# A two-layer attention and mixture-of-experts kernel: 23 tiles of expert rows in place of 24, with the last turn of each loop cut to three slots

## The chip, the cores and the metric

The kernel runs on one core of a Trainium2 chip. The time is the device time of one execution in microseconds (us), taken from the core. Several executions are made of each kernel and the median is given. The core has five engines, each with a queue of its own: PE (TensorE, matmuls), ACT (ScalarE), DVE (VectorE), POOL (GpSimd) and SP (SyncE, which here only issues transfers). They meet through semaphores alone.

## What is computed

x has 8 batches of 512 tokens with 128 channels, 4096 rows in all. Four layers follow each other, each added to x: a gated power attention, an expert layer, a delta rule layer, and the same expert layer again. The expert layer is the part that matters here:

```python
x = hidden_states.reshape(-1, c)                 # 4096 rows of 128
gates = softmax((x @ w_red) @ wg_n.T)            # 8 experts
idx = argmax(gates, axis=1)                      # one expert for each row
h = gelu(x @ w1[idx] + b1[idx])                  # 512 wide
out = (h @ w2[idx] + b2[idx]) * gates[idx]
```

## The kernel before

The function `experts` is called twice, with f = 0 (expert stage 0, some 430 to 560 us into the span) and f = 1 (expert stage 1, the last of the kernel, from about 960 us). In both, the rows are first sorted by expert into the DRAM tensor `xs_dram` by indirect transfers that POOL issues. Each expert has an area there, filled to a multiple of ST = 256 rows. A tile is 256 rows of one expert. How many tiles each expert has is known only on the chip, so DVE computes two tables of NS entries, `texp` (the expert of a tile) and `t_row` (its first row), and the program works on NS tiles whatever the routing is. With 4096 rows and 8 experts no routing needs more than floor((4096 + 8 * 255) / 256) = 23 tiles. NS is that number rounded up to a multiple of SLOTS = 4, which is 24. Entries past the last real tile name the last expert and rows of an idle area, and their results go to rows of `ys_dram` that nobody reads.

A tile is worked on in slot q of turn r: its number is 4r + q, and NR = 6 turns make the stage. All buffers that transfers fill (`xs`, `w1s`, `w2s`, `bs`, `yo`) have four slots. What one tile needs, engine by engine:

- SP, `rows(r, q)`: loads the tile's first row number into a register (L1387), waits until the slot's rows of four tiles ago were turned by PE (`x_ps`, L1389) and their row numbers were read by DVE (`who_done`, L1390), and issues the transfer of the rows (L1391). `weights(r, q)`: loads the expert's number (L1373), issues w1 (L1376), w2 (L1380) and the biases (L1382).
- PE, `turn_x` (L1786, two transposes), `up` (L1796), `down` (L1806), `turn_y` (L1817, two transposes). They are software-pipelined: one pass of `run` for slot q does `turn_x` of the next tile, `up` of this one, `turn_y` of the tile two back, and `down` of the tile one back.
- ACT copies the turned rows (`x_copy`, L1505) and makes the four GELUs (L1514).
- DVE, `y_bias` (L1692), then in `y_out` the two small operations that make the target rows (L1701 and L1704, which counts `who_done`), and the copy of the result (L1707).
- POOL, `give_back`: two indirect transfers to `ys_dram` (L1439).

The order is set by the queues alone. Each engine has the first turn written out, then a hardware loop (`Fori`) over the turns. On PE and ACT the last turn is written out again (`run(NR - 1, last=True)`), without `turn_x` in its last slot; PE then empties its pipeline with `turn_y`, `down` and `turn_y`. On SP, DVE and POOL the loop goes to the last turn. The lines of SP's loop:

```python
            with sp.Fori(0, NR - 1) as r:
                for q in range(SLOTS):
                    rows(r + 1, q, True)
                    weights(r + 1, q, True)
```

After stage 0 all engines meet at a barrier (L1276), and the delta rule layer reads all of `ys_dram`. After stage 1, SP waits for all four slots' `ys_out`, reads `ys_dram` back (L1414), DVE adds it to x (L1721), and x is stored (L1419).

Of the kernel before, what the change touches and what calls it, by code (L numbers as in the profile page):

```python
# [38 lines left out]
ST = 256  # L39
SLOTS = 4  # L40
NS = -(-((B * T + E * (ST - 1)) // ST) // SLOTS) * SLOTS
NR = NS // SLOTS
SPAN = SLOTS * ST
# [1231 lines left out]
def experts(nc, x, xs_dram, ys_dram, s, keep, f, w_red, wg, w1, b1, w2, b2, out):  # L1275
    with ExitStack() as ctx:  # L1276
# [91 lines left out]
        def _(sp):  # L1368
# [35 lines left out]
            rows(0, SLOTS - 1, f > 0)  # L1404
            with sp.Fori(0, NR - 1) as r:
                for q in range(SLOTS):
                    rows(r + 1, q, True)
                    weights(r + 1, q, True)

            if f == 1:  # L1410
                for q in range(SLOTS):
                    sp.wait_ge(ys_out[q], 16 * NC2 * NR * (f + 1))
                for k in range(B):
# [10 lines left out]
        def _(pool):  # L1424
# [16 lines left out]

            with pool.Fori(0, NR) as r:
                for q in range(SLOTS):
                    give_back(r, q)

        @block.scalar
        def _(act):
# [59 lines left out]
            def gelu(r, q, late=True):  # L1507
                g = NS * f + SLOTS * r + q
                act.wait_ge(s["h_ps"], g + 1)
                act.wait_ge(ws_in[q], 48 * (NR * f + r + 1))  # L1510
                if late:
                    act.wait_ge(s["y_ps"], g - 1)
                for n in range(NF):
                    ins = act.activation(hs[:, q % 2, n, :],  # L1514
                                         bH[:, 2 * (q % 2) + n // 2, ST * (n % 2):ST * (n % 2) + ST],
                                         ACT.Gelu, bias=bs[:, q, n:n + 1])
                ins.then_inc(s["h_sb"], 1)

            def run(r, late=True, last=False):
                for q in range(SLOTS):  # L1520
                    if not (last and q == SLOTS - 1):
                        x_copy(*before_slot(r, q, -1), late or q >= 1)
                    gelu(r, q, late or q >= 2)
# [8 lines left out]
        def _(dve):  # L1532
# [153 lines left out]
            def y_bias(r, q, late=True):  # L1686
                g = NS * f + SLOTS * r + q
                dve.wait_ge(s["y_ps"], g + 1)
                dve.wait_ge(ws_in[q], 48 * (NR * f + r + 1))
                if late:  # L1690
# [4 lines left out]
            def y_out(r, q, late=True):  # L1695
                g = NS * f + SLOTS * r + q
                if late:

                    dve.wait_ge(ys_out[q], 16 * NC2 * (NR * f + r))
                dve.wait_ge(xs_in[q], 16 * (NR * f + r + 1))  # L1700
                dve.tensor_scalar(aside[:, q, :], xs[:, q, :, C], float(B * T), float(ST * q), ALU.is_ge, ALU.mult)\  # L1701
# [8 lines left out]
            for q in range(SLOTS):  # L1710
                y_bias(0, q, late=f > 0 or q >= 2)
                y_out(0, q, late=f > 0)
            with dve.Fori(1, NR) as r:
                for q in range(SLOTS):
                    y_bias(r, q)
                    y_out(r, q)
            for i in range(NT if f == 1 else 0):
                if i % TT == 0:
# [6 lines left out]
        def _(pe):  # L1725
# [53 lines left out]
            def turn_x(r, q, late=True):  # L1779

                g = NS * f + SLOTS * r + q
                pe.wait_ge(xs_in[q], 16 * (NR * f + r + 1))
                if late:
# [5 lines left out]
            def up(r, q, late=True):  # L1789
                g = NS * f + SLOTS * r + q  # L1790
                pe.wait_ge(ws_in[q], 48 * (NR * f + r + 1))
                pe.wait_ge(s["x_sb"], g + 1)
# [27 lines left out]
            def run(r, first=False, last=False):  # L1820

                for q in range(SLOTS):
                    if not (last and q == SLOTS - 1):
                        turn_x(*before_slot(r, q, -1))
# [11 lines left out]
            run(NR - 1, last=True)  # L1836
            turn_y(NR - 1, SLOTS - 2)
            down(NR - 1, SLOTS - 1)
            turn_y(NR - 1, SLOTS - 1)


def delta_rule(nc, x, ys_out, ys, keep, row_in, row_done, counted, Wq, Wk, Wv, Wgamma, Wf, Wg1, Wg2, Wo, norm_w):
    with ExitStack() as ctx:
# [135 lines left out]
        def _(sp):  # L1979
            for q in range(SLOTS):  # L1980
                sp.wait_ge(ys_out[q], 16 * NC2 * NR)
            for k in range(B):
# [741 lines left out]
```

## Time and profile before

| | |
|---|---|
| median of 3 runs | 1151.78 us (1148.69 to 1154.24) |
| the profiled execution | 1151.33 us, its span 1149.5 us |
| mean granted clock of TensorE | 0.856 of full speed |
| PE busy (matmuls) | 853.0 us, 74% of the span |
| DVE busy | 761.6 us, 66% |
| POOL busy | 560.9 us, 49% |
| ACT busy | 536.1 us, 47% |

The span goes from the first to the last instruction; the profiled execution's own time lies 1.8 us above it. Busy shares are means over four layers with different limits. For this change only the two expert stages matter, so the rows further down come from these two stretches. A queue's name with a q (SPq) means the instructions of the engine's sequencer: issues of transfers, register and branch instructions.

### The profile page before, as it was taken

The page shows a single profiled execution, that of the slowest core. Times are in us where ns is not written, and L with a number is a line of the kernel's source. Part 1 is how long each engine was busy: PE and PEld are TensorE (multiplying, and loading weights), DVE is VectorE, ACT ScalarE, POOL GpSimd, SP SyncE. Part 2 cuts the span into 40 slices and gives each one's busy share as a digit, 9 for nine tenths or more (in the row PEclk, how much of TensorE's full clock was granted, in tenths as well). Part 3 has the DMA queues.
Part 4 walks back from the last instruction along what each step waited for, and adds up shares of the span by engine and source line. Part 5 has one row for each costly group of instructions (what it writes and reads, how often), then busy time and mean ns, then how long its engine had stood idle before and what let it go on. Part 6 is the DMA issues. An engine that isn't in the chain of part 4 may idle for free. (4 is left out here: it accounts for less than half of the span.)

```text
span 1149.5 us, 26726 instructions
## 1 busy us (share of the span) xinstructions
PE 853.0 (74%) x9326; PEld 630.0 (55%) x9326; DVE 761.6 (66%) x1722; ACT 536.1 (47%) x1219; POOL 560.9 (49%) x698
## 2 busy tenths in 40 slices
PE   3678888888888753999188999468678574629992
PEld 2455555656555533778124786156556463528781
DVE  7577687786877741222364889999999997612224
ACT  4577677576675722444055220255555531214440
POOL 4466557576575631444550010277777841534442
PEclk9998898798887966999688999878878985559997
DMA  5343141331413004666338400000020110156665
GB/s 161 112 155 98 60 162 46 125 109 59 161 52 119 11 11 139 180 186 185 102 60 106 74 1 0 0 1 0 0 73 0 36 38 10 38 156 171 189 191 165
DMA packets 129207, 101.80 MB, mean 89 GB/s; under 512 B 20640, under 2 KB 116832, under 8 KB 129056
## 3 DMA queue, kind: packets, MB, share of 16 engines
q1 hardware_dynamic: 120080, 87.27, 27.5%
q0 software_dynamic: 5120, 10.53, 2.7%
q10 hardware_dynamic: 3904, 2.61, 0.8%
q8 instruction: 68, 1.11, 0.4%
q14 instruction: 35, 0.29, 0.1%
HBM read 57.98 MB, written 35.45 MB: 81 GB/s over the span
## 5 line engine op out<-in xcount | busy, mean ns | idle before, releaser
L796 DVE TENSOR_SCALAR a_mag<-a_pS 128x1024 int32<-128x1024 int32 (+1 forms) x192 | 180.1, 950 | 65.1 <-PE a_pS L1155 63.2
L553 ACT ACTIVATE a_pw<-a_mag,a_eps_a 128x1024 f32<-128x1024 f32 (+1 forms) x192 | 175.5, 935 | 57.5 <-DVE a_mag L796 52.0
L1439 POOL DMA_INDIRECT ys_dram<-f_yo,f_who x96 | 91.9, 957 | 137.8 <-DVE f_yo L1707 121.1
L416 POOL TENSOR_TENSOR a_pw<-a_pw,a_decay 128x256 f32<-128x256 f32 x128 | 93.1, 728 | 104.7 <-ACT a_pw L553 104.3
L1155 PE MATMUL a_pS<-a_qf,a_kf 64*64 64x192 bf16 (+3 forms) x1536 | 111.2, 270 | 5.0 <-DVE a_mag L796 3.5
L1514 ACT ACTIVATE f_hs<-f_bH,f_bs 128x256 f32<-128x256 f32 x192 | 75.2, 474 | 67.5 <-issue 35.1
L2617 PE MATMUL d_c<-d_pb_p,ident 128*128 128x256 f32 x256 | 72.3, 452 | 41.9 <-POOL d_pb_p L2100 41.9
L1187 PE MATMUL a_pOff<-a_pw,a_vo 128*18 128x64 f32 x3584 | 97.1, 242 | 2.3 <-issue 2.3
L1796 PE MATMUL f_bH<-f_xsT,f_w1s 128*128 128x256 f32 x384 | 94.1, 389 | 0.0
L1692 DVE TENSOR_SCALAR f_ysT<-f_bY,f_bs 128x256 f32<-128x256 f32 x48 | 23.2, 484 | 106.9 <-PE f_bY L1806 87.6
L1806 PE MATMUL f_bY<-f_hs,f_w2s 128*128 128x256 f32 x384 | 90.8, 379 | 0.0
L2617 PEld LDWEIGHTS d_c<-d_pb_p,ident 128*128 128x128 f32 x256 | 58.6, 232 | 56.1 <-issue 39.0
L1155 PEld LDWEIGHTS a_pS<-a_qf,a_kf 64*64 64x64 bf16 x1536 | 65.3, 115 | 30.8 <-DVE a_mag L796 7.8
L2617 PE MATMUL d_c<-d_pb_d,ident 128*128 128x256 f32 (+1 forms) x256 | 64.8, 419 | 22.0 <-POOL d_pb_d L2100 22.0
L1187 PEld LDWEIGHTS a_pOff<-a_pw,a_vo 128*18 128x18 f32 x3584 | 69.2, 109 | 17.5 <-issue 13.9
L2094 POOL TENSOR_TENSOR d_pb_p<-d_Q,d_s_sb 128x512 f32<-128x512 f32 x32 | 37.3, 1166 | 83.1 <-ACT d_s_sb L2202 83.1
L1796 PEld LDWEIGHTS f_bH<-f_xsT,f_w1s 128*128 128x128 f32 x384 | 71.1, 195 | 9.1 <-issue 0.2
L1806 PEld LDWEIGHTS f_bY<-f_hs,f_w2s 128*128 128x128 f32 x384 | 69.2, 190 | 7.7
L2617 PEld LDWEIGHTS d_c<-d_pb_d,ident 128*128 128x128 f32 x256 | 53.2, 220 | 33.5 <-POOL d_pb_d L2100 24.8
L1707 DVE COPY f_yo<-f_bO 128x256 f32<-128x256 f32 x48 | 20.4, 425 | 71.9 <-PE f_bO L1817 57.1
L364 POOL TENSOR_TENSOR a_vo<-a_vd,a_reach 128x1008 f32<-128x1008 f32 (+6 forms) x56 | 65.9, 1191 | 1.1 <-issue 1.1
L2198 ACT ACTIVATE d_G<-d_c,d_g_ahead 128x64 f32<-128x64 f32 x64 | 24.0, 375 | 71.2 <-DVE d_og L2435 71.2
(395 smaller groups left out, 1837.6 us busy)
## 6 DMA issues: line engine op xcount, KB each, us to landing
parts_scratch<-a_parts SPq DMA_DIRECT2D x32, 384.0 KB
f_w1s<-in_L_ffn_w_dram SPq DMA_DIRECT2D x48, 256.0 KB
f_w2s<-in_L_ffn_w_dram SPq DMA_DIRECT2D x48, 256.0 KB
a_kf<-parts_scratch SPq DMA_DIRECT2D x16, 512.0 KB, 5.7
a_qf<-parts_scratch SPq DMA_DIRECT2D x16, 512.0 KB, 7.7
f_xs<-xs_dram SPq DMA_DIRECT2D x48, 129.0 KB
parts_scratch<-a_parts SPq DMA_DIRECT2D x16, 256.0 KB
xs_dram<-blank ACTq DMA_DIRECT2D x16, 129.0 KB
```

What stands on the lines that cost most here:

```text
L364: pool.tensor_tensor(vo[:, vo_at(j, j + 1):vo_at(j, j + 1) + n, :, :], vd[:, k, j, :, :].unsqueeze(1).broadcast_to([P, n, NP, 18]), reach[ ...
L416: pool.tensor_tensor(own, own, decay[:, k, m, hf:NP:2, :], ALU.mult)\
L553: act.activation(pw[:, n % 4, 0:N], mag[:, n % 3, 0:N], ACT.Square, bias=eps_a[:, 0:1])\
L796: dve.tensor_scalar(mag[:, n % 3, 0:2 * N].bitcast(I32).rearrange("p (l t) -> p l t", l=2), pS[:, 2 * (n % 2):2 * (n % 2) + 2, 0:N].bitcas ...
L1155: ins = pe.matmul(pS[lo:hi, 2 * (n % 2) + Q // 2, at:at + L * (end - first)], kf[lo:hi, k, p, L * m:L * m + L], qf[lo:hi, k, p, L * first: ...
L1187: ins = pe.matmul(pOff[lo:hi, L * i:L * i + L], vo[:, vo_at(m, i), p, :], wi, start=False, stop=(m == NM - 2), skip_group_check=True)
L1439: pool.indirect_dma_start(ys_dram[f][:, :], bass.IndirectOffsetOnAxis(ap=who[:, q, a:a + 1], axis=0), yo[:, q, a, :], None).then_inc(ys_ou ...
L1514: ins = act.activation(hs[:, q % 2, n, :], bH[:, 2 * (q % 2) + n // 2, ST * (n % 2):ST * (n % 2) + ST], ACT.Gelu, bias=bs[:, q, n:n + 1])
L1796: ins = pe.matmul(bH[:, 2 * (q % 2) + n // 2, ST * (n % 2):ST * (n % 2) + ST], w1s[:, q, P * n:P * n + P], xsT[:, q % 2, :], start=True, s ...
L1806: ins = pe.matmul(bY[:, 0:ST], w2s[:, q, n, :], hs[:, q % 2, n, :], start=(n == 0), stop=(n == NF - 1))
L2094: pool.tensor_tensor(po[:, 0:8], Q[:, :, :, bass.ds(c, 1)].rearrange("p k j c -> p k (j c)").unsqueeze(3) .broadcast_to([P, HD, CH, HD]), ...
L2617: ins = pe.matmul((c5, c6)[a][:, 0:64 * chunks].rearrange("p (c x) -> p c x", x=64), ident[:, :], po[:, k], start=(k == 0), stop=(k == 15))
```

## The change

NS becomes 23, without the rounding. NR stays 6 (rounded up), `LEFT` = 3 is the number of slots in the last turn, and `TURNS` = [6, 6, 6, 5] says how often each slot is used; it takes the place of NR in the counts that are waited for. The tables `texp` and `t_row` have 23 entries. In both expert stages SP's loop makes 4 turns in place of 5, POOL's 5 in place of 6, DVE's 4 in place of 5, and each is followed by three slots that are written out. PE and ACT keep their loops and lose the last slot of their last turn, which was written out before.

```diff
@@ -38,8 +38,10 @@
-NS = -(-((B * T + E * (ST - 1)) // ST) // SLOTS) * SLOTS
-NR = NS // SLOTS
+NS = (B * T + E * (ST - 1)) // ST
+NR = -(-NS // SLOTS)
+LEFT = NS - SLOTS * (NR - 1)
+TURNS = [NR if q < LEFT else NR - 1 for q in range(SLOTS)]
...
@@ -1402,14 +1404,17 @@
-            with sp.Fori(0, NR - 1) as r:
+            with sp.Fori(0, NR - 2) as r:
                 for q in range(SLOTS):
                     rows(r + 1, q, True)
                     weights(r + 1, q, True)
+            for q in range(LEFT):
+                rows(NR - 1, q, True)
+                weights(NR - 1, q, True)
...
-                    sp.wait_ge(ys_out[q], 16 * NC2 * NR * (f + 1))
+                    sp.wait_ge(ys_out[q], 16 * NC2 * TURNS[q] * (f + 1))
...
-            with pool.Fori(0, NR) as r:
+            with pool.Fori(0, NR - 1) as r:
                 for q in range(SLOTS):
                     give_back(r, q)
+            for q in range(LEFT):
+                give_back(NR - 1, q)
...
@@ -1517,8 +1524,8 @@
             def run(r, late=True, last=False):
-                for q in range(SLOTS):
-                    if not (last and q == SLOTS - 1):
+                for q in range(LEFT if last else SLOTS):
+                    if not (last and q == LEFT - 1):
                         x_copy(*before_slot(r, q, -1), late or q >= 1)
                     gelu(r, q, late or q >= 2)
...
@@ -1710,10 +1717,13 @@
-            with dve.Fori(1, NR) as r:
+            with dve.Fori(1, NR - 1) as r:
                 for q in range(SLOTS):
                     y_bias(r, q)
                     y_out(r, q)
+            for q in range(LEFT):
+                y_bias(NR - 1, q)
+                y_out(NR - 1, q)
...
@@ -1819,8 +1829,8 @@
             def run(r, first=False, last=False):
 
-                for q in range(SLOTS):
-                    if not (last and q == SLOTS - 1):
+                for q in range(LEFT if last else SLOTS):
+                    if not (last and q == LEFT - 1):
                         turn_x(*before_slot(r, q, -1))
...
             run(NR - 1, last=True)
-            turn_y(NR - 1, SLOTS - 2)
-            down(NR - 1, SLOTS - 1)
-            turn_y(NR - 1, SLOTS - 1)
+            turn_y(NR - 1, LEFT - 2)
+            down(NR - 1, LEFT - 1)
+            turn_y(NR - 1, LEFT - 1)
```

How the instructions stand at the end of expert stage 0. First PE, from `turn_x` of the third tile of the last turn on. The first instruction of each piece is shown, with the semaphores that it waits for (f_bA: `turn_x`, f_bH: `up`, f_bO: `turn_y`, f_bY: `down`). Before:

```order
L1786 MATMUL f_bA<-ident,f_xs 128x128 [waits f_x_sb,f_xs_in2]
L1796 MATMUL f_bH<-f_xsT,f_w1s 128x256 [waits f_h_sb,f_x_sb,f_ws_in1]
L1817 MATMUL f_bO<-ident,f_ysT 128x128 [waits f_o_sb,f_y_sb]
L1806 MATMUL f_bY<-f_hs,f_w2s 128x256 [waits f_y_sb,f_h_sb]
L1786 MATMUL f_bA<-ident,f_xs 128x128 [waits f_x_sb,f_xs_in3]
L1796 MATMUL f_bH<-f_xsT,f_w1s 128x256 [waits f_h_sb,f_x_sb,f_ws_in2]
L1817 MATMUL f_bO<-ident,f_ysT 128x128 [waits f_o_sb,f_y_sb]
L1806 MATMUL f_bY<-f_hs,f_w2s 128x256 [waits f_y_sb,f_h_sb]
L1796 MATMUL f_bH<-f_xsT,f_w1s 128x256 [waits f_h_sb,f_x_sb,f_ws_in3]
L1817 MATMUL f_bO<-ident,f_ysT 128x128 [waits f_o_sb,f_y_sb]
L1806 MATMUL f_bY<-f_hs,f_w2s 128x256 [waits f_y_sb,f_h_sb]
```

And after the change, from the same place:

```order
L1796 MATMUL f_bA<-ident,f_xs 128x128 [waits f_x_sb,f_xs_in2]
L1806 MATMUL f_bH<-f_xsT,f_w1s 128x256 [waits f_h_sb,f_x_sb,f_ws_in1]
L1827 MATMUL f_bO<-ident,f_ysT 128x128 [waits f_o_sb,f_y_sb]
L1816 MATMUL f_bY<-f_hs,f_w2s 128x256 [waits f_y_sb,f_h_sb]
L1806 MATMUL f_bH<-f_xsT,f_w1s 128x256 [waits f_h_sb,f_x_sb,f_ws_in2]
L1827 MATMUL f_bO<-ident,f_ysT 128x128 [waits f_o_sb,f_y_sb]
L1816 MATMUL f_bY<-f_hs,f_w2s 128x256 [waits f_y_sb,f_h_sb]
L1827 MATMUL f_bO<-ident,f_ysT 128x128 [waits f_o_sb,f_y_sb]
L1816 MATMUL f_bY<-f_hs,f_w2s 128x256 [waits f_y_sb,f_h_sb]
```

One pass of `turn_x`, `up`, `turn_y` and `down` is gone; the lines are later by 10 (one `up` and one `turn_x` with its wait for f_xs_in3 are missing), and the emptying of the pipeline has the same form.

Second SP, from the end of its loop in stage 0. Before, the loop's branch is followed by the branch to the barrier and by the delta rule layer's first transfers:

```order
L1382 ISA
L1382 DMA f_bs<-bT 128x5
L1405 REGISTER_ALU
L1405 COMPARE_AND_BRANCH
L1276 UNCONDITIONAL_BRANCH
L1978 UNCONDITIONAL_BRANCH [waits barrier_Pool_Activation_PE_DVE_SP_release]
L1983 DMA d_LL<-ys_dram 128x4x128 [waits f_ys_out2,f_ys_out3,f_ys_out1,f_ys_out0]
```

After the change, the loop's branch is followed by the first written-out slot (f_xs is the rows, f_w1s and f_w2s the weights, TENSOR_LOAD reads the table entry):

```order
L1384 ISA
L1384 DMA f_bs<-bT 128x5
L1407 REGISTER_ALU
L1407 COMPARE_AND_BRANCH
L1389 TENSOR_LOAD f_t_row
L1389 ISA x2
L1393 ISA [waits f_who_done,f_x_ps]
L1393 DMA f_xs<-xs_dram 128x2x129
L1375 TENSOR_LOAD f_texp
L1375 ISA x2
L1378 ISA [waits f_h_sb]
L1378 DMA f_w1s<-in_L_ffn_w_dram 128x512
```

The written-out slot has no REGISTER_ALU ahead of its table loads, since the entry's address is a constant; two more such slots follow it, and then the branch to the barrier.

## Rows read from the trace of the kernel before

**Rows 1.** Busy times by window: a stretch of each expert stage's loop

```profile
core 0: us, PE busy (x) PEld busy (x) DVE busy (x) ACT busy (x) POOL busy (x), PEclk, DMA share, GB/s
460.00:540.00 80.00, 76.33 (x382) 63.34 (x381) 22.14 (x77) 37.09 (x97) 36.37 (x38) 1.00 0.68 188
...
1023.00:1120.00 97.00, 90.85 (x444) 74.88 (x445) 23.77 (x84) 43.86 (x113) 38.31 (x40) 0.96 0.62 176
```

**Rows 2.** Timeline of PE, stage 0: `turn_x` (L1786) of tiles 19, 20 and 23

```profile
524.60 0.38 PE L1786 MATMUL f_bA<-ident,f_xs 128*128 128x128 f32 x2
...
529.31 0.43 PE L1786 MATMUL f_bA<-ident,f_xs 128*128 128x128 f32 x2 [0.65 <-DMA f_xs<-xs_dram]
...
541.29 0.38 PE L1786 MATMUL f_bA<-ident,f_xs 128*128 128x128 f32 x2
```

**Rows 3.** Timeline of PE, stage 1: `turn_x` of tiles 19 to 23, one `up`, one `down`

```profile
1100.93 0.40 PE L1786 MATMUL f_bA<-ident,f_xs 128*128 128x128 f32 x2
...
1105.57 0.43 PE L1786 MATMUL f_bA<-ident,f_xs 128*128 128x128 f32 x2 [0.56 <-DMA f_xs<-xs_dram]
...
1109.54 0.38 PE L1786 MATMUL f_bA<-ident,f_xs 128*128 128x128 f32 x2
...
1109.76 1.89 PE L1796 MATMUL f_bH<-f_xsT,f_w1s 128*128 128x256 f32 x8
...
1111.71 1.89 PE L1806 MATMUL f_bY<-f_hs,f_w2s 128*128 128x256 f32 x8
...
1113.49 0.44 PE L1786 MATMUL f_bA<-ident,f_xs 128*128 128x128 f32 x2
...
1117.49 0.44 PE L1786 MATMUL f_bA<-ident,f_xs 128*128 128x128 f32 x2
```

**Rows 4.** Timeline, stage 1: DVE's target rows and SP's issue of rows, tiles 20 and 22

```profile
1101.91 0.16 DVE L1704 TENSOR_TENSOR f_who<-f_aside,f_xs 128x2 int32<-128x2 f32 x1
...
1103.34 0.36 SPq L1391 DMA_DIRECT2D f_xs<-xs_dram  x1
...
1110.34 0.16 DVE L1704 TENSOR_TENSOR f_who<-f_aside,f_xs 128x2 int32<-128x2 f32 x1
...
1111.30 0.38 SPq L1391 DMA_DIRECT2D f_xs<-xs_dram  x1
```

**Rows 5.** The chain that ended last, SP's loop turn in stage 1 (start, us, what)

```profile
1093.55 0.27 SPq L1387
...
1101.62 0.23 issue
1101.85 0.07 SPq L1405
...
1101.96 0.40 SPq L1387
```

**Rows 6.** Timeline at the ends of stage 0 and stage 1

```profile
555.30 0.96 POOL L1439 DMA_INDIRECT ys_dram<-f_yo,f_who  x1 [0.30 <-issue]
560.83 0.20 POOL L2037 MEMSET d_ones<- 128x128 f32 x1 [4.57 <-POOLq L1276]
...
1131.55 0.96 POOL L1439 DMA_INDIRECT ys_dram<-f_yo,f_who  x1 [0.30 <-issue]
1133.87 5.40 SPq L1414 DMA_DIRECT2D f_ya<-ys_dram  x8
```

**Rows 7.** The barrier's line L1276 on POOL's queue (durations min/median/max in ns)

```profile
L1276 POOLq DRAIN  x2: 6179/7314/8450, 554.4 to 1130.7; - x2
```

**Rows 8.** Timeline of DVE, stage 1: one operation on the tables of 24 tiles

```profile
1007.51 0.35 DVE L1622 TENSOR_REDUCE f_texp_f<-f_past 128x24 f32<-128x192 f32 x1
```

**Rows 9.** The chain that ended last, SP's first slots of stage 1

```profile
1017.57 0.70 SPq L1373
```

**Rows 10.** Timeline of SP, stage 1: the fourth slot of the first turn

```profile
1027.63 0.35 SPq L1376 DMA_DIRECT2D f_w1s<-in_L_ffn_w_dram  x1
...
1028.61 0.50 SPq L1382 DMA_DIRECT2D f_bs<-bT  x1
```

More of the change, by code:

```diff
@@ L1509, in gelu @@
                 act.wait_ge(s["h_ps"], g + 1)
-                act.wait_ge(ws_in[q], 48 * (NR * f + r + 1))
+                act.wait_ge(ws_in[q], 48 * (TURNS[q] * f + r + 1))
                 if late:
@@ L1688, in y_bias @@
                 dve.wait_ge(s["y_ps"], g + 1)
-                dve.wait_ge(ws_in[q], 48 * (NR * f + r + 1))
+                dve.wait_ge(ws_in[q], 48 * (TURNS[q] * f + r + 1))
                 if late:
@@ L1697, in y_out @@
                 if late:
-                    dve.wait_ge(ys_out[q], 16 * NC2 * (NR * f + r))
-                dve.wait_ge(xs_in[q], 16 * (NR * f + r + 1))
+                    dve.wait_ge(ys_out[q], 16 * NC2 * (TURNS[q] * f + r))
+                dve.wait_ge(xs_in[q], 16 * (TURNS[q] * f + r + 1))
                 dve.tensor_scalar(aside[:, q, :], xs[:, q, :, C], float(B * T), float(ST * q), ALU.is_ge, ALU.mult)\
@@ L1781, in turn_x @@
                 g = NS * f + SLOTS * r + q
-                pe.wait_ge(xs_in[q], 16 * (NR * f + r + 1))
+                pe.wait_ge(xs_in[q], 16 * (TURNS[q] * f + r + 1))
                 if late:
@@ L1790, in up @@
                 g = NS * f + SLOTS * r + q
-                pe.wait_ge(ws_in[q], 48 * (NR * f + r + 1))
+                pe.wait_ge(ws_in[q], 48 * (TURNS[q] * f + r + 1))
                 pe.wait_ge(s["x_sb"], g + 1)
@@ L1980, in _ @@
             for q in range(SLOTS):
-                sp.wait_ge(ys_out[q], 16 * NC2 * NR)
+                sp.wait_ge(ys_out[q], 16 * NC2 * TURNS[q])
             for k in range(B):
```

## The prediction

> **What bounds the kernel now.** I read the busy times by window first. In both expert loops PE is busy for 76.33 of 80 us and 90.85 of 97 us, some 94 to 95%, at a granted clock of 1.00 and 0.96 of full speed, which is the upper of its two levels nearly throughout; DVE is busy for a quarter, ACT and POOL for less than half, and the 16 DMA engines for 0.62 to 0.68 of the time [rows 1]. So a tile costs what PE needs for it, as long as nothing makes PE wait.
>
> The timeline of PE shows that cost as the distance from one `turn_x` to the next. In stage 0 three distances of the last turn take 541.29 - 529.31 = 11.98 us, 3.99 each [rows 2]. In stage 1 they take 1117.49 - 1105.57 = 11.92 us, 3.97 each, and nearly all of it is PE's work: `up` and `down` take 1.89 each, and the two pairs of transposes fill the rest [rows 3].
>
> Then the place where PE does wait. Tile 20 is the first slot of the last turn. In stage 0 it comes 529.31 - 524.60 = 4.71 us after the one before it, and in stage 1 1105.57 - 1100.93 = 4.64 us, both times with a wait for the rows' transfer (0.65 and 0.56 us) [rows 2, 3]. The timeline of DVE and SP tells why. For tile 22 SP issues the rows 0.80 us after DVE has read the row numbers of four tiles ago (1110.34 + 0.16 to 1111.30). For tile 20 it takes 1.27 us (1101.91 + 0.16 to 1103.34) [rows 4]. The 0.47 us between are SP's loop turn, and the chain shows its pieces: 0.23 us after the compare and branch in which nothing runs, 0.07 us for a register operation of L1405, and a table load of 0.40 us where it is 0.27 elsewhere [rows 5]. SP is thus close behind PE, and a late row transfer reaches PE at once.
>
> Last the ends. In stage 0 the last indirect transfer is issued by 555.30 + 0.96 = 556.26 us, and the next layer's first POOL instruction comes 4.57 us later, after POOL's own drain of the barrier [rows 6, 7]. In stage 1 SP reads the results back at 1133.87, 2.32 us after POOL began its last issue [rows 6]. Both follow the last tile, and I see nothing beside them that would hold the next step back.
>
> **The change part by part.** *The tile itself.* Two transposes, `up`, `turn_y`, `down` of one tile leave PE's queue in each stage, and the emptying of the pipeline keeps its form, as the order on PE shows. The cost removed is one distance: 3.99 us in stage 0 and 3.97 us in stage 1, together 7.96 us. Its transfers (rows, w1, w2, biases in, two indirect transfers out), its GELUs and its DVE operations lie beside PE's work of other tiles and go with it. They are worth nothing more, except if transfers were slowing each other; in the last turn nothing is behind them.
>
> *SP's last turn written out.* Tile 20 is now reached by leaving the loop, not by going round. The compare and branch stays. What can go is the 0.23 us, the 0.07 us and the excess of the table load, 0.40 - 0.27 = 0.13 us, 0.43 us in all [rows 5]. The bounds are 0 (leaving the loop costs what going round does) and 0.43 us a stage; it can't be more, since PE's own excess at tile 20 is 0.67 and 0.72 us (4.64 - 3.97, 4.71 - 3.99). I take 0.35, near the upper end, because the pieces belong to going round, and because the written-out slots lack two register operations each. That is 0.7 us for both stages. The semaphore waits keep their order, so no wait is new; rows and weights of tile 20 to 22 stand in the queue as before.
>
> For this place there is a price on a page: the Trainium skill, Advanced Engine Details and Errata, section Control Flow Timing, has some 51 ns for a branch and 108 ns for a compare and branch. No row here shows so little for a whole turn: the trace has 0.23 us of standstill alone. By that page, as an estimate, a turn would be worth at most 0.11 us, and the sum would be some 0.5 us smaller, 1143.3 us.
>
> *POOL and DVE written out.* POOL's queue waits for DVE's copy in each tile and DVE's for PE, with idle time of over half in the windows, so a turn more or less is hidden; if that cover were gone, the price would be a turn like SP's, 0.47 us. Their waits name counts that hold one use less of the fourth slot, which changes no order.
>
> *The tables.* Eight DVE operations run over 23 entries in place of 24. One of the longest takes 0.35 us [rows 8], so a 24th of each is 0.015 us at most, 0.12 us a stage. Shorter ones are worth less and part of each is fixed; I take 0.05 us for both stages.
>
> *Sum.* 7.96 + 0.70 + 0.05 = 8.7 us. Against the profiled execution's 1151.33 us that makes 1142.6 us; the median of the runs shown is 0.45 us higher. I put the forecast at 1142.8 us, 0.77% below the median.
>
> **The rivals.** *The new code is fetched late.* The three written-out slots of SP, DVE and POOL run once, so the first pass meets code that no earlier turn has brought in. The trace has no row of such a stall; the widest gap at a jump to other code is the 4.57 us before stage 0's next layer, most of which is the barrier's drain [rows 6, 7]. With one such stall on SP in one stage, and none of it hidden, the time is 1142.8 + 4.57 = 1147.4 us, with one in both 1151.9. Against it: the fourth slot of the first turn in stage 1 is new code too, and its issues take 0.35 and 0.50 us, with 1.5 us from the first one's start to the last one's end [rows 10]. Chance 0.14, most of it for one stall.
>
> On this the Trainium skill has a rule, in Runtime: NRT & Kernel Launch, section Instruction fetch mechanics: instructions are brought in by blocks in order, mostly hidden, and only a taken branch out of the blocks held forces a fetch. By that rule this rival would not happen at the three slots, and the jump to the barrier would cost what it does now. The trace's fourth slot agrees, the jump itself can't be told from the drain.
>
> *Stage 0 gives nothing.* POOL's drain lasts 6.18 and 8.45 us in the two stages [rows 7]. If in stage 0 it is ended by something other than the last tiles' transfers, the barrier stays where it is and only stage 1 counts: 3.97 + 0.35 = 4.3 us, which is 4.3 us less than the sum, so 1147.1 us. Against it: the drain ends 4.4 us after the last indirect issue, with no other transfer under way that the program still waits for. Chance 0.06.
>
> *Nothing changes.* The 24th tile could be cheaper than the others, as idle rows and a repeated expert. PE's distances at tile 23 speak against it (3.95 to 4.00 us), and the chip knows no difference between the tiles. With the two distances gone from the sum the time is 1142.8 + 7.96 = 1150.8 us. Chance 0.03.
>
> *Slower.* In the first slots of stage 1, SP's queue crawls: an instruction of a table load takes 0.70 us [rows 9], and so do its neighbours, where the whole load takes 0.27 in the loop [rows 5]. Why, no row says. If the new slots crawled so, the 13 instructions that the order shows for a slot would take 9.1 us in place of the 3.97 that PE leaves for it. Three slots make 3 x 5.13 = 15.4 us. In one stage alone that gives 1142.8 + 15.4 = 1158.2 us. It decides from 0.3 us an instruction on (3.97 / 13). Against it: the slots right behind the crawl, from 1027.63 on, are quick again [rows 10]. Chance 0.04.
>
> *A larger gain*, 1140 us or less: a run at the lower end of the spread, which is 5.5 us wide in three runs before. Chance 0.06.
>
> **How the numbers follow.** The forecast has the remaining 0.67. Its own range is 1140.5 to 1145.0: the turn's bounds make 0.9 us, the spread of medians about 1.5 us to each side. To hold 8 in 10 it must reach to the case with one stall or with one stage, at 1147.3, so 1139.8 to 1148.0. Faster by over 0.5% means under 1146.0: the forecast, the larger gain and a small part of the stalls, 0.75. Within 0.5%: the stalls, stage 0 lost, nothing changed, 0.20. Slower by over 0.5%: 0.05. A difference of 0.5% is about what a measurement of this kernel can tell from no change.
>
> **What would show it.** In the new trace, the distances of `turn_x` are 3.97 to 3.99 us in the last turn as before, there are 46 pairs of them in place of 48, and the barrier of stage 0 stands 4.3 us earlier. SP's issue for tile 20 comes some 0.9 us after DVE's operation, not 1.27, and PE's distance there is 4.2 to 4.4 us. I am wrong if PE waits at tiles 20 to 22 for over 1 us (fetch), if POOL's drain grows by what the tile gave, or if the layers between change their length.

## The result and the profile after

The change takes 1143.36 us (median of 6 runs, 1141.62 to 1146.01) against 1151.53 us (6 runs, 1148.69 to 1154.24). The ratio is 0.993, with a 95% interval of 0.9916 to 0.9943: 8.2 us, 0.7%, faster. The forecast was 1142.8 us.

The page of the profiled execution, its head and first rows:

```profile
span 1139.8 us, 26534 instructions
## 1 busy us (share of the span) xinstructions
PE 842.8 (74%) x9286; PEld 622.0 (55%) x9286; DVE 758.1 (67%) x1714; ACT 533.6 (47%) x1209; POOL 557.3 (49%) x694
```

PE has 40 matmuls fewer, 20 a stage, which is one tile. The span is 9.7 us shorter than in the one profiled execution of before. The medians say 8.2, so some 1.5 us of the difference between these two traces is chance. The first `turn_x` of stage 0 already stands 1.28 us earlier (447.85 against 449.13). Over the traces of all the kernels in this document that point lies anywhere from 446.1 to 450.1 us, so this says nothing of the change.

The timeline of PE, `turn_x` (now L1796) of tiles 19, 20 and 22 in stage 0, answers to [rows 2]; the first POOL instruction behind the barrier answers to [rows 6]:

```profile
522.00 0.43 PE L1796 MATMUL f_bA<-ident,f_xs 128*128 128x128 f32 x2
...
526.05 0.43 PE L1796 MATMUL f_bA<-ident,f_xs 128*128 128x128 f32 x2
...
534.04 0.38 PE L1796 MATMUL f_bA<-ident,f_xs 128*128 128x128 f32 x2
...
548.05 0.96 POOL L1444 DMA_INDIRECT ys_dram<-f_yo,f_who  x1 [0.30 <-issue]
553.41 0.20 POOL L2047 MEMSET d_ones<- 128x128 f32 x1 [4.40 <-POOLq L1278]
```

Tile 20 comes 4.05 us after tile 19, where it was 4.71, and PE no longer waits there. Tile 22 is the last. In stage 1 the same tiles stand like this, and the read of the results answers to the last of [rows 6]:

```profile
1094.96 0.43 PE L1796 MATMUL f_bA<-ident,f_xs 128*128 128x128 f32 x2
...
1099.04 0.43 PE L1796 MATMUL f_bA<-ident,f_xs 128*128 128x128 f32 x2
...
1107.01 0.38 PE L1796 MATMUL f_bA<-ident,f_xs 128*128 128x128 f32 x2
...
1121.01 0.96 POOL L1444 DMA_INDIRECT ys_dram<-f_yo,f_who  x1 [0.30 <-issue]
...
1123.37 5.11 SPq L1419 DMA_DIRECT2D f_ya<-ys_dram  x8
```

Again 4.08 us to tile 20, where it was 4.64. The two places on DVE and SP that answer to [rows 4] are, for tile 20 in stage 0:

```profile
522.95 0.16 DVE L1711 TENSOR_TENSOR f_who<-f_aside,f_xs 128x2 int32<-128x2 f32 x1
...
523.86 0.62 SPq L1393 DMA_DIRECT2D f_xs<-xs_dram  x1
```

SP issues the rows 0.75 us after DVE's operation. In the same stage before, it was 1.32 us (525.59 + 0.16 to 527.07). The stretches of the kernel add up as follows, each one's length before and after, in us:

| stretch | before | after | difference |
|---|---|---|---|
| start to first `turn_x` of stage 0 | 449.13 | 447.85 | -1.28 |
| first to last `turn_x`, stage 0 | 92.16 | 86.19 | -5.97 |
| last `turn_x` to the barrier's end (L2037, now L2047) | 19.54 | 19.37 | -0.17 |
| barrier to first `turn_x` of stage 1 | 465.47 | 465.64 | +0.17 |
| first to last `turn_x`, stage 1 | 91.19 | 87.96 | -3.23 |
| last `turn_x` to the end of the span | 32.01 | 32.79 | +0.78 |

The gain lies where tiles are worked on and, beside the chance start, nowhere else. It is 6 us in one stage and 3 in the other, though the same tile is gone from both. In stage 0 a part is one wait that the trace of before has at tile 8 (5.00 us after tile 7) and the trace of the change has not (3.99 us). So beside the tile something else moves by a microsecond or more from stage to stage. The experiments ask what.

### The profile page after: what moved, and what is told of

Same layout as the page of the kernel before. It is cut to its first block and busy times, and to the rows that moved or that the text cites. A ratio compares the mean times of both kernels' runs of the same rounds, so it can differ in the third digit from the quotient of the medians.

```text
span 1139.8 us, 26534 instructions
## 1 busy us (share of the span) xinstructions
PE 842.8 (74%) x9286; PEld 622.0 (55%) x9286; DVE 758.1 (67%) x1714; ACT 533.6 (47%) x1209; POOL 557.3 (49%) x694
## 5 line engine op out<-in xcount | busy, mean ns | idle before, releaser
L1444 POOL DMA_INDIRECT ys_dram<-f_yo,f_who x92 | 88.0, 957 | 133.2 <-DVE f_yo L1714 117.1
L1521 ACT ACTIVATE f_hs<-f_bH,f_bs 128x256 f32<-128x256 f32 x184 | 72.2, 475 | 67.0 <-PE f_bH L1806 34.0
L1806 PE MATMUL f_bH<-f_xsT,f_w1s 128*128 128x256 f32 x368 | 91.7, 393 | 0.0
L1816 PE MATMUL f_bY<-f_hs,f_w2s 128*128 128x256 f32 x368 | 87.0, 379 | 0.0
L1816 PEld LDWEIGHTS f_bY<-f_hs,f_w2s 128*128 128x128 f32 x368 | 66.4, 190 | 7.3
```

The source lines that it names most:

```text
L1444: pool.indirect_dma_start(ys_dram[f][:, :], bass.IndirectOffsetOnAxis(ap=who[:, q, a:a + 1], axis=0), yo[:, q, a, :], None).then_inc(ys_ou ...
L1521: ins = act.activation(hs[:, q % 2, n, :], bH[:, 2 * (q % 2) + n // 2, ST * (n % 2):ST * (n % 2) + ST], ACT.Gelu, bias=bs[:, q, n:n + 1])
L1806: ins = pe.matmul(bH[:, 2 * (q % 2) + n // 2, ST * (n % 2):ST * (n % 2) + ST], w1s[:, q, P * n:P * n + P], xsT[:, q % 2, :], start=True, s ...
L1816: ins = pe.matmul(bY[:, 0:ST], w2s[:, q, n, :], hs[:, q % 2, n, :], start=(n == 0), stop=(n == NF - 1))
```

## The experiments

My theory: two parts, a tile at PE's distance in each stage (8 us), and SP's loop turn at tile 20 (0.7 us forecast, 0.66 + 0.56 = 1.22 us in the trace). Rivals: that the second part comes from DVE's or POOL's loops; that it is chance; that the 24th tile's transfers had a price of their own; and that the gain is in the written-out code rather than in the tile.

**One part alone: SP's last turn written out, 24 tiles.**

```diff
-            with sp.Fori(0, NR - 1) as r:
+            with sp.Fori(0, NR - 2) as r:
                 for q in range(SLOTS):
                     rows(r + 1, q, True)
                     weights(r + 1, q, True)
+            for q in range(SLOTS):
+                rows(NR - 1, q, True)
+                weights(NR - 1, q, True)
```

> 24 tiles as before, with SP's last turn alone written out. If the change's gain has a part in the form of SP's code (my theory), tile 20 comes 4.0 to 4.1 us after tile 19 in both stages, where it was 4.71 and 4.64, and the time is about 1.2 us below the kernel before. If the part at tile 20 came from the missing tile or from DVE's and POOL's loops, tile 20 stays at 4.6 to 4.7 us and the time is that of before.

Measured: tile 20 comes 4.06 and 4.04 us after tile 19. Its timeline in stage 0 (`turn_x` of tiles 19 and 20, here L1789):

```profile
521.89 0.43 PE L1789 MATMUL f_bA<-ident,f_xs 128*128 128x128 f32 x2
525.95 0.43 PE L1789 MATMUL f_bA<-ident,f_xs 128*128 128x128 f32 x2
```

The time is 1151.42 us, a ratio of 1.0002 (0.9989 to 1.0014). The local effect is there in the trace, both times; the time doesn't show it. By its interval, a gain of 1.3 us is still possible, so 1.2 us can just be hidden in it.

**The other part alone: the last turns of DVE and POOL written out, 24 tiles.**

```diff
-            with pool.Fori(0, NR) as r:
+            with pool.Fori(0, NR - 1) as r:
...
+            for q in range(SLOTS):
+                give_back(NR - 1, q)
...
-            with dve.Fori(1, NR) as r:
+            with dve.Fori(1, NR - 1) as r:
...
+            for q in range(SLOTS):
+                y_bias(NR - 1, q)
+                y_out(NR - 1, q)
```

> 24 tiles as before, with the last turns of DVE and POOL written out and SP's loop left. My theory: nothing moves, tile 20 stays at 4.6 to 4.7 us after tile 19 and the time is within noise of before. The rival, that DVE's turn and not SP's is the one that makes the rows late: tile 20 falls to about 4.0 us.

Measured: 1152.12 us, ratio 0.999 (0.9976 to 1.0003); tile 20 after 4.25 us in stage 0 and 4.78 in stage 1:

```profile
1106.46 0.43 PE L1791 MATMUL f_bA<-ident,f_xs 128*128 128x128 f32 x2 [0.67 <-DMA f_xs<-xs_dram]
```

In stage 1 the wait stays, as expected. In stage 0 it is mostly gone although SP's loop is untouched. So a turn of SP doesn't always reach PE, and a single distance in a single trace proves less than I took from it.

**23 tiles, but SP keeps its loop and loads 24.** Nobody uses the last load. The table has 24 entries again, and the counts that the other engines wait for are those of six turns in every slot (not shown).

```diff
-            with sp.Fori(0, NR - 2) as r:
+            with sp.Fori(0, NR - 1) as r:
                 for q in range(SLOTS):
                     rows(r + 1, q, True)
                     weights(r + 1, q, True)
-            for q in range(LEFT):
-                rows(NR - 1, q, True)
-                weights(NR - 1, q, True)
+            sp.wait_ge(xs_in[SLOTS - 1], 16 * NR * (f + 1))
+            sp.wait_ge(ws_in[SLOTS - 1], 48 * NR * (f + 1))
...
```

> 23 tiles on PE, ACT, DVE and POOL as in the change, but SP keeps its old loop and loads a 24th tile's rows and weights that nobody uses. My theory: the tile's PE work alone gives 3.99 + 3.97 = 7.96 us, and tile 20 stays at 4.6 to 4.7 us, so about 1143.6 us, some 0.8 to 1.2 us above the change. The rival, that the transfers of the 24th tile cost time of their own: the time is over 2 us above the change.

Measured: 1143.43 us, ratio 0.992 (0.9902 to 0.9939); tile 20 after 4.14 and 4.72 us, the latter with a wait of 0.60 us for the rows. The wait at tile 20 stayed in one stage only, against my expectation. The time is that of the change to 0.1 us by the medians, which come from two sets of runs; a median of four runs that spread over 2.6 us can't tell a difference of 1 us. So the tile's work on the engines is the gain, its transfers have no price that can be measured, and the 0.7 us that I had put on SP's form does not show between these two, though it isn't ruled out either.

**One tile less again: NS = 22.** This kernel would lose rows under a routing that needs 23 tiles; it serves the measurement alone.

```diff
-NS = (B * T + E * (ST - 1)) // ST
+NS = (B * T + E * (ST - 1)) // ST - 1
```

> The change with one tile less again: 22 tiles, the last turn has two slots (a routing that needs 23 tiles would lose rows, so a part of the computation may be left out). My theory: a tile is worth its distance on PE, 3.9 to 4.1 us a stage wherever it is taken, so 7.9 to 8.2 us less than the change, about 1135.4 us. The rival, that most of the change's gain is in the written-out code and only little in the tile: less than 6 us.

Measured: 1134.76 us (1133.45 to 1135.87), ratio 0.9848 (0.9822 to 0.9874). The change itself, beside it on the same chip:

> The change itself once more, on the chip of the other three, as the kernel to compare them with: 1143.4 us, 8 us below before. Distance to tile 20 of 4.0 to 4.1 us in both stages if its loss of SP's turn is steady; 4.6 or more in one of them if that was chance.

Measured: 1144.0 us (1137.79 to 1145.74), ratio 0.9928 (0.9903 to 0.9954), tile 20 after 3.97 and 4.21 us, nearer to the steady case than to the 4.6 of the other. So the second tile brings 9.2 us by these medians, 8.6 by the change's first 1143.36. Both are above the 7.9 to 8.2 us expected. The five runs of the change spread over 8 us, though, and the stages' own stretches in the traces (first to last `turn_x`, mean of three traces of the change) shrink by 7.6 us. The average distance from tile 4 to the last is 4.12 and 4.20 us in the kernel with 22 tiles, which makes 8.3 us a tile. That the gain is the tile's distance, and not the written-out code, stands. But the distance that counts is the average, 4.1 to 4.2, not the best three of a turn.

**All of SP's turns written out.** The waits in the middle turns ask for this one.

```diff
-            with sp.Fori(0, NR - 2) as r:
-                for q in range(SLOTS):
-                    rows(r + 1, q, True)
-                    weights(r + 1, q, True)
-            for q in range(LEFT):
-                rows(NR - 1, q, True)
-                weights(NR - 1, q, True)
+            for i in range(SLOTS, NS):
+                rows(i // SLOTS, i % SLOTS, True)
+                weights(i // SLOTS, i % SLOTS, True)
```

> The change with all of SP's turns written out. My theory: each loop turn of SP costs PE 0.5 to 0.7 us at one tile of a turn; the profile of the change shows three such waits in stage 0 (tiles 6, 12, 16) and two or three in stage 1, so 2 us a stage go, 3 to 4 us in all, about 1139.8 us. The rival, that new code is fetched late once it fills many blocks: SP's issues show gaps of over 1 us that the loop has not, and the time is the change's or above it.

Measured: 1136.21 us (1135.74 to 1136.99), ratio 0.9858 (0.9842 to 0.9875), 7 us below the change. That is twice what I expected. The chain that ended last says what had been misread. By line, over stage 1's loop, first in the change, then with SP written out:

```profile
by line: PE f_bH L1806 17.5%; issue 15.2%; PE f_bY L1816 15.1%; SPq L1384 7.6%; SPq L1393 7.3%; SPq L1389 6.8%; SPq L1375 6.8%; SPq L1378 5.9%; SPq L1382 5.7%; SPq L1391 3.3%; PE f_bA L1796 3.1%; DMA f_xs<-xs_dram 2.4%; PE f_bO L1827 1.8%; 
```

```profile
by line: PE f_bH L1802 41.9%; PE f_bY L1812 41.8%; PE f_bA L1792 5.7%; PE f_bO L1823 5.2%; DMA f_xs<-xs_dram 3.2%; issue 0.9%; SPq L1393 0.7%; DVE f_who L1707 0.2%; DVE f_aside L1704 0.2%; DVE f_ysT L1695 0.1%; DVEq L1692 0.1%; DVEq L1694 0
```

In the change over half of the chain (the SPq lines and "issue") runs through SP's queue and its gaps; with SP written out, 95% of it is PE. The stages' stretches shrink by 6.2 us against the mean of three traces of the change. So most of the 7 us lies where SP's form was changed. The windows of a middle stretch of both stages agree (columns as in [rows 1]); first the change, then SP written out:

```profile
460.00:530.00 70.00, 68.35 (x341) 56.52 (x339) 19.45 (x68) 33.23 (x85) 32.53 (x35) 1.00 0.70 192
1030.00:1100.00 70.00, 68.53 (x338) 56.12 (x337) 19.49 (x68) 33.23 (x85) 31.70 (x34) 1.00 0.65 185
```

```profile
460.00:530.00 70.00, 69.82 (x357) 59.63 (x356) 20.84 (x72) 34.16 (x89) 34.47 (x36) 1.00 0.73 201
1030.00:1100.00 70.00, 69.62 (x353) 59.12 (x352) 20.41 (x70) 34.22 (x88) 33.60 (x35) 1.00 0.72 199
```

PE's busy time grows by only 1.1 to 1.5 of 70 us, but its matmuls by 15 to 16 of 340. The records seem to put part of the waiting into the matmuls and not into idle time. Busy shares of 94 to 98% had hidden a loss of 4% (4.11 to 3.95 us a tile in stage 0, see the table below). SP now has a little time to wait. Who SP's queue waited for between 455 and 530 us (us in total, times, longest), first in the change, then with SP written out:

```profile
SPq L1392 <- DVE f_who L1711: 4.4, 1, 4.4
```

```profile
SPq L1392 <- DVE f_who L1707: 7.1, 6, 4.6
```

The longest wait is there in both; the other five are new, 2.5 us together. The rival's sign does not appear: apart from the longest wait for DVE, SP's queue stands still for at most 0.87 us at a time in this stretch and 0.72 us between 1022 and 1095 us, and the change's own loop shows standstills of 0.7 us too. The time fell by twice what was hoped, so new code being fetched late is out as a price here.

**The same edit on the kernel before, 24 tiles.**

```diff
-            with sp.Fori(0, NR - 1) as r:
-                for q in range(SLOTS):
-                    rows(r + 1, q, True)
-                    weights(r + 1, q, True)
+            for i in range(SLOTS, NS):
+                rows(i // SLOTS, i % SLOTS, True)
+                weights(i // SLOTS, i % SLOTS, True)
```

> 24 tiles as before, all of SP's turns written out. With 23 tiles the same edit took 7 us off the change. If SP's issue and not PE sets the pace in the loop, the distances fall to 3.9 us here too and the time is about 1144 us, 8 us below before; a tile is then worth two PE distances of 3.89, so it stands 7.8 us above the 23-tile kernel with SP written out (1136.2). The rival, that the gain hangs together with the missing tile: less than 4 us.

Measured: 1142.9 us (1141.19 to 1146.78), ratio 0.9924 (0.9903 to 0.9945). SP's form alone is worth as much as the whole change (0.9924 against 0.993), and the two ratios multiplied give 0.9855, which is what both together measured (0.9858). The tile is worth 6.7 us by these medians, which come from two sets of runs, against 7.8 expected; the stages' stretches of the two traces differ by 7.9 us.

**SP's loop with two turns in a pass.** This halves the branches and keeps every slot's register operations. The tables have 24 entries again, since the loop's own bounds reach that far (not shown).

```diff
-            with sp.Fori(0, NR - 2) as r:
-                for q in range(SLOTS):
-                    rows(r + 1, q, True)
-                    weights(r + 1, q, True)
+            with sp.Fori(0, NR - 2, 2) as r:
+                for k in (1, 2):
+                    for q in range(SLOTS):
+                        rows(r + k, q, True)
+                        weights(r + k, q, True)
...
```

> The change, but SP's loop holds two turns in a pass and makes two passes; the tables have 24 entries again, so that the loop's bounds hold. It keeps the register operations of every slot and halves the branches. If the branches alone are what costs, one of two waits per stage of 0.6 to 0.7 us goes and the time is some 1.5 us below the change. If the register operations in each slot are what costs, the distances stay at 3.97 to 4.1 us between the branches, and of the 7 us that writing out brought under a quarter is won. If both cost the same, it is about 3 us.

Measured: 1135.29 us, ratio 0.9925 (0.99 to 0.995). But in this set of runs the kernel before took 1144.14 us (7 runs, 1141.02 to 1146.82), not 1152, and the change itself did not run there. So the 1.5 or 3 us below the change can't be read from it. Two more kernels ran beside it: all five engines' turns written out (SP's as above, not shown again), and SP's turns written out again.

```diff
-            with pool.Fori(0, NR - 1) as r:
+            for r in range(NR - 1):
...
-            with act.Fori(1, NR - 1) as r:
+            for r in range(1, NR - 1):
...
-            with dve.Fori(1, NR - 1) as r:
+            for r in range(1, NR - 1):
...
-            with pe.Fori(1, NR - 1) as r:
+            for r in range(1, NR - 1):
```

> The change with the turns of all five engines written out in both expert stages. With SP alone written out the distances are 3.89 to 4.1 us with some 1 us a stage above 23 times 3.89. If the other engines' turns make that rest, about 1.5 us go, 1134.7 us. The rival, that it is the first transfers and not the turns, or that so much new code is fetched late: within 1 us of SP alone written out (1136.2), or above it.

> The change with SP's turns written out, once more, beside the other two: 1136 to 1137 us, a ratio to before of 0.986 to 0.988.

Measured: 1135.35 us, ratio 0.9926 (0.9902 to 0.9951), with all engines, and 1134.92 us, ratio 0.9924 (0.9899 to 0.9948), with SP alone. The 1.5 us that I expected from the other engines' turns did not come: their loops cost nothing that can be measured, and neither does the five engines' much longer code. The expectation for SP alone, 0.986 to 0.988, was missed in the ratio and not in the time: its denominator had moved.

What is different on this chip? The page of the profile seems to say that transfers land sooner: it has 5.7 us for the 512 KB load a_qf where the change's page has 7.9. It would be wrong to read it so. The kernel with 24 tiles and SP written out has 5.7 us on its page too, and it ran where the kernel before takes 1153.26 us. The landings in the traces agree with each other as well: a pair of these loads, the second issued at 158.38 us in the change and at 157.17 us here, has landed 4.9 us later in both. The page's median leaves out a semaphore whose landings the trace holds incompletely, and in the change's trace that is the one of the quicker half. The rows' transfers do not seem to land sooner here either (2.3 us against 1.7 on the pages of the same kernel, SP written out, the second again from incomplete landings).

What the traces do show is on SP's own queue. The register operation just ahead of each rows' transfer (duration min/median/max in ns), SP written out in both cases, first on the chip where the kernel before takes 1152 us, then on this one:

```profile
L1393 SPq MOVE f_xs<-xs_dram x18: 3/29/707, 461.3 to 528.5; - x18
```

```profile
L1393 SPq MOVE f_xs<-xs_dram x18: 29/29/38, 462.7 to 529.4; - x18
```

In all eleven other traces, the longest register operation of SP in each stage's loop lasts 0.57 to 0.72 us; in the three traces of this chip none lasts over 0.16 us. From the end of the wait to the end of the rows' issue SP needs 0.78 us on average in the first of these two traces and 0.57 us in the second. So SP is quicker where the kernel before is 5 to 9 us faster, and with SP written out the gain of the place is only 1.3 us (1136.21 to 1134.92). That fits a queue that has slack in one form and none in the other. Why SP's operations take so long on the other chips, and whether the chip itself is the reason, no run shows. And since the whole gain of tile and form together is only 0.76% there, against 1.42%, the 7 us of SP's form seem to hold only where SP is slow.

**Both again on one chip.** Since the loop of two turns had been timed only where the kernel before is quick, it ran once more beside the change.

> The change once more, beside SP's loop of two turns on one chip. In two of the three sets of runs so far the kernel before took 1152 to 1153 us, in the third 1144. If this set is of the first kind, the change takes 1143 to 1144 us, its ratio 0.992 to 0.994. If it is of the second kind, in which SP's loop seems to cost little, the change takes 1135 to 1137 us.

> SP's loop with two turns in a pass, where the kernel before takes 1152 us: 1141.9 us if the branches alone cost (1.5 us below the change), above 1142 with distances of 3.97 to 4.1 us between the branches if the register operations do, 1136 to 1137 us as with SP written out if it is neither but the shortness of the loop's pass. Where the kernel before takes 1144 us, all of these lie within 1.5 us and this tells nothing.

Measured: the change 1143.38 us (1141.06 to 1143.78), ratio 0.9937 (0.9915 to 0.9959); two turns in a pass 1138.77 us (1137.87 to 1141.47), ratio 0.9906 (0.9884 to 0.9928). The kernel before took 1149.08 us beside them. The expectation's three cases were 1141.9 for branches alone, above 1142 for register operations alone and 1136 to 1137 for neither. The result lies between. Halving the branches wins 4.6 us by the medians and 3.5 by the means, but the two stages' stretches in the traces shrink by only 2.1 us (85.53 and 86.60 us, against means of 86.24 and 87.95 over three traces of the change), where SP written out shrinks them by 6.2. So the branches' share is between a third and two thirds of SP's form, and 2.1 us for four branches is little above my 0.47 us a turn. The rest can be the remaining branch or the register operations: the change and the loop of two turns run 19.7 instructions of SP for each tile in stage 0's loop, SP written out 17.4. The runs don't divide it.

The average distance of `turn_x` from tile 4 to the last, worked out from the first and last row of each trace, sets the kernels side by side:

| kernel | stage 0, us | stage 1, us |
|---|---|---|
| before (24 tiles) | 4.21 | 4.16 |
| the change | 4.11 | 4.15 |
| the change, second and third time | 4.09, 4.12 | 4.16, 4.18 |
| SP's last turn written out, 24 tiles | 4.06 | 4.14 |
| DVE's and POOL's last turns written out, 24 tiles | 4.21 | 4.20 |
| 23 tiles, SP loads 24 in its loop | 4.14 | 4.24 |
| two turns in a pass | 4.07 | 4.09 |
| two turns in a pass, on the quick chip | 3.96 | 3.97 |
| SP written out | 3.95 | 3.98 |
| SP written out, 24 tiles | 3.96 | 3.96 |
| SP written out, on the quick chip | 3.92 | 3.94 |
| all engines written out, on the quick chip | 3.93 | 4.00 |

PE's own work for a tile shows as 3.89 us, the least distance from tile 4 on in all of them. SP written out is the version that beats both kernels, by 1.4% against before, and by 0.8% on the quick chip.

## Why the prediction was right, and where it was off

**The tile's distance.** The step was 3.99 + 3.97 = 7.96 us. It held: the time fell by 8.2 us, 23 tiles with SP's loop kept show the same time, and a second tile off brings 8.6 to 9.2 us. The reason given for it, that PE's work is what bounds the loop, was wrong for much of it. PE's work is 3.89 us; the average distance is 4.1 to 4.2, since SP's queue sets the pace for a good part. The prediction had read the three distances after the wait at tile 20 (3.97 to 3.99), which lie between the two. All of these give nearly the same price for a tile, 7.8 to 8.4 us, and that is luck: with a larger loss on SP's queue the same reading would have priced the tile too low. The sum of 8.7 us came near 8.2 in part because the tile was priced 0.4 us below the average distances of before (4.21 + 4.16), and SP's form 0.7 us above what the times show of it. (8.98 us below the median is 0.78%, where the prediction has 0.77.)

**SP's last turn written out.** I took 0.35 us a stage from bounds of 0 and 0.43. In the trace tile 20 came 0.66 and 0.56 us sooner. One pair of traces is little, since the distance varies: with SP's loop going round it is 4.14 to 4.78 us (mean 4.54, three traces), with the last turn written out 3.97 to 4.21 (mean 4.07, three traces of the change and the one with 24 tiles). The means differ by 0.47 us, just what the prediction had read as a turn. When the loop is left, the trace shows 0.045 us of standstill behind the branch, where going round showed 0.13 us in stage 0 and 0.23 in stage 1; the prediction's row was the larger one. The mechanism is there, then, near its upper bound. In the time it can't be told: alone on the kernel before it gives a ratio of 1.0002 (0.9989 to 1.0014), and the kernel with SP's loop kept is as fast as the change. Of the signs named beforehand, SP's issue came after 0.75 us (0.9 forecast), tile 20 after 4.05 and 4.08 (4.2 to 4.4 forecast), and the barrier of stage 0 stood 7.4 us earlier (4.3 forecast), 1.3 us of it from the start and some 1 us from the wait at tile 8.

**POOL and DVE at nothing.** Nothing speaks against it: 0.999 (0.9976 to 1.0003) when they are written out alone, so up to 0.24% stays possible, and no gain when all engines are (on the quick chip).

**The ends.** Right. Stage 0's barrier followed the last tile (19.54 and 19.37 us from the last `turn_x`), so the rival that stage 0 gives nothing is out. POOL's drain kept its length (6.15 and 8.42 us, before 6.18 and 8.45 [rows 7]):

```profile
L1278 POOLq DRAIN  x2: 6147/7284/8422, 547.0 to 1120.0; - x2
```

**New code fetched late.** It didn't happen, at three slots, at nineteen of SP's, or with all engines. What the Trainium skill says in Runtime: NRT & Kernel Launch, section Instruction fetch mechanics, that code in a row is brought in ahead and mostly hidden, agrees with these runs: all engines written out take 1135.35 us, SP alone 1134.92.

**The crawl of SP's queue** in the first slots of stage 1 [rows 9] is in the change's trace too: the first three slots' issues go from 1002.24 to 1015.26 us. It didn't spread to the new slots. In the traces of the quick chip it is missing: with SP written out the same issues go from 998.37 to 1004.61 us there, and from 999.90 to 1012.31 on the chip of the 1152 us. So it seems to belong with the slow register operations of SP shown above. Its cause stays open, and no experiment tried it.

**Stage 1's smaller difference** (3.23 us for 5.97) is partly the clock. Tiles 2 and 3 come after 3.86 and 4.31 us, where it was 3.26 and 3.67 before, 1.24 us in all. The transposes of tile 2 last 0.63 us in place of 0.38:

```profile
1024.14 0.63 PE L1796 MATMUL f_bA<-ident,f_xs 128*128 128x128 f32 x2
```

The windows of the first and the next stretch of the stage say why (the clock is third from the end). First the change, then before:

```profile
1018.00:1024.00 6.00, 4.38 (x12) 3.37 (x13) 0.00 (x0) 0.77 (x2) 0.00 (x0) 0.50 0.57 161
1024.00:1029.00 5.00, 5.00 (x23) 4.24 (x22) 0.29 (x1) 3.55 (x10) 0.00 (x0) 0.86 0.05 14
```

```profile
1026.00:1031.00 5.00, 4.13 (x14) 3.17 (x15) 0.00 (x0) 0.77 (x3) 0.00 (x0) 0.59 0.59 159
1031.00:1036.00 5.00, 5.00 (x27) 4.32 (x26) 0.72 (x3) 3.78 (x10) 0.00 (x0) 1.00 0.10 25
```

Both begin after 22 us of an idle PE at half speed, the lower level. Before, the upper one is granted by 1031; in the change only in the course of the next 5 us. Both kinds occur with 24 and with 23 tiles: one more trace of the change starts stage 1 with 3.50 and 3.67 us, and the kernel with SP's last turn written out and 24 tiles with 3.89 and 4.16. So this is chance and no effect of the change.

**What would have given more.** My reading of what bounds the kernel stopped at PE's busy share. The chain over stage 1's loop (1031 to 1117 us) has SP's lines ahead of PE's:

```profile
by line: issue 25.9%; SPq L1382 10.3%; SPq L1387 9.5%; PE f_bH L1796 8.1%; SPq L1373 8.1%; SPq L1376 7.8%; PE f_bY L1806 7.6%; SPq L1380 7.5%; SPq L1391 5.0%; SPq L1389 2.5%; DMA f_xs<-xs_dram 2.4%; SPq L1390 2.3%; PE f_bA L1786 1.4%; PE f_
```

That would have pointed at the 7 us of SP's form.

## What to carry to other kernels

A tile that is taken off a software-pipelined loop is worth the average distance between tiles, whatever engine sets it; read it from the first to the last tile, not from the best three. When an engine is 95% busy, look at the chain of waits over the loop before calling it the bound: time in which matmuls wait inside the pipeline seems to count as busy. A queue that only issues transfers can be nearly full without any busy share telling so, and then every operation in its loop counts; if the trip count is known, writing it out costs little code. Before a difference between two sets of runs is put down to a row of the page, compare that row in every trace: one kernel of this document had the "quick" landing time at the slow place.

## What the runs showed of the hardware

- Behind the compare and branch of SP's loop, the kernel before showed 0.13 us of standstill in stage 0 and 0.23 in stage 1, and 0.045 us where the loop is left (in the change). Going round cost 0.47 us at tile 20 on average. Four turns a stage made into two brought 3.5 to 4.6 us in the time and 2.1 us in the two stages; made into none, and with fewer register operations in each slot, 7.2 and 6.2 us. The turns of PE, ACT, DVE and POOL showed no cost where they were written out (1135.35 against 1134.92 us).
- PE's records showed 4.7% more matmuls in a stretch (357 for 341) at 2% more busy time (69.82 for 68.35 us), with SP's turns written out.
- The longest register operations of SP lasted up to 0.72 us in the loops of eleven traces, and never over 0.16 us in the three traces of one chip. There the kernel before was 5 to 9 us faster than elsewhere, the kernel with SP written out 1.3 us.
